# A vision-transformer block on one core: padded small products, other instruction orders, and both normalisations moved from VectorE to ScalarE

## The reference

```python
h = x.reshape(8, 1024, 29) @ tok_W + positions                 # 128 channels
z = layernorm(h)                                               # (h - mean) / sqrt(var + eps)
Q, K, V = (split_heads(z @ W + b) for W, b in ...)             # 8 heads of 16
attn = softmax((Q @ K.T + causal_mask) / 4)
h = h + (attn @ V) @ Wo + bo
y = layernorm(layernorm(h)) * ln_scale + ln_bias               # the second one inside the feed-forward part
shared = swiglu(y @ shared_in.T) @ shared_out.T + shared_out_b
# routing: argmax over 2 groups, softmax over the group's 4 experts, the top 2 of them, renormalised
routed = sum_e comb[:, e] * (swiglu(y @ expert_in.T) @ expert_out[e].T) + counts @ expert_out_bias
out = h + shared + routed
```

## Time and profile before

| | before |
|---|---|
| median of 3 runs | 1126.03 us |
| the profiled execution | 1126.66 us, its span 1124.9 us |
| granted TensorE clock, mean | 0.972 |
| TensorE busy | 1024.5 us (91%), 5632 products |
| VectorE busy | 787.9 us (70%) |
| ScalarE busy | 602.6 us (54%) |
| GpSimd busy | 324.3 us (29%) |
| DMA, mean over the span | 31 GB/s |

### The profile page before, as it was taken

One profiled execution on the slowest core, in us unless ns is written; L12 is line 12 of the kernel. 1 busy time (PEld: TensorE's weight loads), 2 busy tenths in 40 slices (PEclk: granted clock), 3 DMA queues, 4 the chain that ended last, 5 costly groups with the idle time before them and its releaser, 6 DMA issues.

```text
span 1124.9 us, 17182 instructions
## 1 busy us (share of the span) xinstructions
PE 1024.5 (91%) x5632; PEld 673.1 (60%) x5632; DVE 787.9 (70%) x2438; ACT 602.6 (54%) x1363; POOL 324.3 (29%) x466
## 2 busy tenths in 40 slices
PE   2688998999989998999989999999989999899966
PEld 1444665666657665676657665675656666576544
DVE  4578667785778767976687857877668857887133
ACT  1124654466645765556644666557644566457633
POOL 5211313123232323224132233313232232222233
PEclk9999999899989999999999999999989999999989
DMA  3520224004130044002140042200350040400000
GB/s 115 72 32 2 30 32 69 1 1 68 25 46 1 1 69 69 2 1 47 23 70 1 2 69 39 32 1 16 55 69 1 1 64 13 59 1 2 10 10 9
DMA packets 28808, 34.66 MB, mean 31 GB/s; under 512 B 5418, under 2 KB 15568, under 8 KB 28592
## 3 DMA queue, kind: packets, MB, share of 16 engines
q1 hardware_dynamic: 28720, 33.57, 19.7%
HBM read 3.61 MB, written 4.19 MB: 7 GB/s over the span
## 4 chain that ended last, share of the span: by engine, by line
PE 71%; DVE 11%; ACT 6%; DMA 4%; issue 3%; SPq 3%; POOL 1%; ACTq 0%; POOLq 0%; DVEq 0%
PE bank_p L495 13%; PE bank_s L470 13%; PE bank_w L513 10%; PE bank_f L598 4%; PE bank_f L600 4%; DVE mx_far L682 4%; PE bank_f L599 4%; PE bank_m L564 3%; SPq L366 2%; PE bank_f L418 2%; ACT sel_act L995 2%; PE bank_f L420 2%; PE bank_f L419 2%; DMA q_stack<-mrow_l 2%; ACT pt L933 2%
## 5 line engine op out<-in xcount | busy, mean ns | idle before, releaser
L933 ACT ACTIVATE pt<-bank_p 128x512 f32<-128x512 f32 (+3 forms) x768 | 353.6, 490 | 299.6 <-PE bank_p L495 282.4
L470 PE MATMUL bank_s<-k_stack,q_stack 112*128 112x512 f32 (+3 forms) x768 | 285.8, 404 | 30.0 <-DMA q_stack<-qk_l 10.2
L686 DVE CUSTOM_DVE_ANT_0 bank_s<-bank_s,causal 128x384 f32<-128x384 f32 (+3 forms) x512 | 246.9, 505 | 89.8 <-PE bank_s L470 83.9
L495 PE MATMUL bank_p<-q_stack,k_stack 128*128 128x512 f32 (+3 forms) x768 | 262.4, 385 | 14.6 <-ACT pt L933 14.0
L470 PEld LDWEIGHTS bank_s<-k_stack,q_stack 112*128 112x128 f32 x768 | 150.2, 201 | 134.5 <-DVE mx L686 68.4
L495 PEld LDWEIGHTS bank_p<-q_stack,k_stack 128*128 128x128 f32 x768 | 141.5, 194 | 114.4 <-ACT pt L933 90.1
L682 DVE TENSOR_REDUCE mx_far<-bank_s 128x1 f32<-128x512 f32 x256 | 166.4, 684 | 43.6 <-PE bank_s L470 42.4
L1070 POOL TENSOR_SCALAR_AFFINE_SELECT pt<-pt 128x512 f32<-128x512 f32 x128 | 81.1, 636 | 384.8 <-ACT pt L933 384.8
L513 PE MATMUL bank_w<-pt,v 128*32 128x512 f32 (+3 forms) x1536 | 162.9, 500 | 0.0
L598 PE MATMUL bank_f<-wex_h,hid_h 128*128 128x512 f32 x256 | 103.7, 405 | 1.3 <-DVE gate_dve L827 0.8
L600 PE MATMUL bank_f<-wex_h,hid_l 128*128 128x512 f32 x256 | 101.2, 395 | 0.0
(11 more groups left out here) (124 smaller groups left out, 1338.1 us busy)
## 6 DMA issues: line engine op xcount, KB each, us to landing
q_stack<-qk_h SPq DMA_DIRECT2D x64, 128.0 KB, 4.1
k_stack<-qk_h SPq DMA_DIRECT2D x64, 128.0 KB, 5.8
q_stack<-qk_l SPq DMA_DIRECT2D x32, 128.0 KB, 5.2
k_stack<-qk_l SPq DMA_DIRECT2D x32, 128.0 KB, 5.8
out<-h SPq DMA_DIRECT2D x16, 256.0 KB, 2.3
pt<-w_expert SPq DMA_DIRECT2D x1, 1024.0 KB
x_sb<-x_t SPq DMA_DIRECT2D x16, 58.0 KB
pos_sb<-pos SPq DMA_DIRECT2D x1, 512.0 KB
```

The lines of the kernel that those rows point to most:

```text
L470: nc.tensor.matmul(s_bank[s % 2][:, 0:cols], q_stack[0:STACK, half, hd, t % HT * P:(t % HT + 1) * P], k_stack[0:STACK, hd // 2, key_place( ...
L495: nc.tensor.matmul(p_bank[p % 2][:, q0:HALF], k_stack[:, hd // 2, key_place(i, kt // HT), kt % HT * P:(kt % HT + 1) * P], q_stack[:, half, ...
L686: nc.vector.tensor_tensor_reduce(src, src, causal[:, HALF - cols:HALF], 1.0, -3.0e38, ALU.add, ALU.max, mx[:, col:col + 1]).then_inc(s_tak ...
L933: nc.scalar.activation(pt[:, k % PT_SLOTS, j, q0:HALF], p_bank[p % 2][:, q0:HALF], ACT.Exp, scale=0.25).then_inc(exp_done, 1)
```

## The change

- **Orders.** `FIRST`, `WEAVE` and `LAST` take the place of the one table: one order for the first two periods together, one for each of the six full ones, one for the last two together. All strings are new, on all five engines.
- **Steps.** The statistics (`stat1`, `stat2`) and the normalising (`z1`, `z2`) become steps of their own, and routing comes in five pieces where it had three.
- **Normalisations.** ScalarE makes `z` and `z2` as `scale * token + shift` with the scale `rs` and the shift `-mean * rs` per token. GpSimd makes the negated mean and the shift, two more small instructions for each half and norm.
- **Values.** `v` is a split product of three fp32r matmuls per tile (12 of 128 columns) where it was a plain fp32 one (4 matmuls, 8 instructions); `zt` and its copy go.
- **Padding.** `x_sb`, `tokw_sb` are padded with zero rows to 128 partitions, the transposes of the maxima and counts to 128 columns, and the counts of four tiles go through one transpose and one fp32 product of 512 columns with a block-diagonal bias in place of four of each.
- **Buffers.** `pt` has three slots; `gate_act` and `gate_dve`, and `sel_act` and `sel_dve`, become one buffer each.
- **Beginning.** The position table comes in two halves, and TensorE no longer waits for it; ScalarE zeroes half of `q_stack` with four copies; VectorE makes the other new constants.

```diff
-PT_SLOTS = 2
+PT_SLOTS = 3
...
-    PROGRAM[engine] = [(n + image_of(st), st) for n in range(-2, B) for st in period(WEAVE[engine], streams())
-                       if 0 <= n + image_of(st) < B]
+    PROGRAM[engine] = woven(FIRST[engine], -2, -1)
+    for n in range(0, B - 2):
+        PROGRAM[engine] += woven(WEAVE[engine], n)
+    PROGRAM[engine] += woven(LAST[engine], B - 2, B - 1)
...
-                        mm = nc.tensor.matmul(m_bank[:, t * P:(t + 1) * P], zt[:, t * P:(t + 1) * P], wv_sb[:],
-                                              start=True, stop=True)
+                        tok = slice(t * P, (t + 1) * P)
+                        mm = split_mm(m_bank[:, tok], zt_h[:, tok], zt_l[:, tok], wqkv_h[:, 2, :], wqkv_l[:, 2, :])
...
-                nc.tensor.transpose(m_bank[0:ROWS, 0:P], mx[:, u * ROWS:(u + 1) * ROWS], ident[:]).then_inc(m_ready, 1)
+                nc.tensor.transpose(m_bank[:, 0:P], mx[:, u, :], ident[:]).then_inc(m_ready, 1)
...
-                    for t in range(HT):
-                        mm = nc.tensor.transpose(m_bank[0:EXPERTS + 1, t * P:(t + 1) * P], cnt[:, half * HT + t, :],
-                                                 ident[:])
+                    mm = nc.tensor.transpose(m_bank[:, 0:P], cnt[:, tiles(half), :].rearrange("p t e -> p (t e)"), ident[:])
...
-                    for t in range(HT):
-                        nc.tensor.matmul(m_bank[:, t * P:(t + 1) * P], cnt_t[:, t * P:(t + 1) * P], wbias_sb[:],
-                                         start=(t == 0), stop=False)
+                    nc.tensor.matmul(m_bank[:], cnt_t[:], wbias_sb[:], start=True, stop=False)
...
-                if kind == "turn1":
-                    dve.wait_ge(rs_made, n + 1)
-                    if n:
-                        dve.wait_ge(m_ready, after(half_before(i, half)[0], "turn1", 1 - half))
-                    for t in range(HT):
-                        nc.vector.tensor_scalar(z[:, t, :], h[:, slot(i, half), t, :], mv[:, t, 0:1], rs1[:, t:t + 1],
-                                                ALU.subtract, ALU.mult).then_inc(z_made, 1)
...
+                if kind == "z1":
+                    act.wait_ge(rs_made, (n + 1) * LN_STEPS)
+                    if n:
+                        act.wait_ge(m_ready, after(half_before(i, half)[0], "turn1", 1 - half))
+                    for t in range(HT):
+                        nc.scalar.activation(z[:, t, :], h[:, slot(i, half), t, :], ACT.Identity, bias=shift1[:, t:t + 1],
+                                             scale=rs1[:, t:t + 1]).then_inc(z_made, 1)
+                    return
...
-                    nc.scalar.copy(zt[:], m_bank[:]).then_inc(zt_made, 1)
...
+                    pool.wait_ge(rs_made, n * LN_STEPS + 1)
+                    nc.gpsimd.tensor_tensor(shift1[:], minus_mean1[:], rs1[:], ALU.mult).then_inc(rs_made, 1)
```

More of the change, by code:

```diff
@@ L24 @@
 GATE_W = 32
+CNT_W = 32
+XROWS = 32
 ODD = 64
@@ L67, in image_of @@
 def image_of(st):
-    if st[0] in ("emb", "turn1", "ztl", "q", "k", "v", "queries", "keys"):
+    if st[0] in ("emb", "stat1", "z1", "turn1", "ztl", "q", "k", "v", "queries", "keys"):
         return 2
@@ L150, in period, with woven @@
+def woven(weave, *periods):
+    joined = {}
+    for n in periods:
+        for name, stream in streams(n).items():
+            joined.setdefault(name, []).extend((n + image_of(st), st) for st in stream if 0 <= n + image_of(st) < B)
+    left = {name: iter(stream) for name, stream in joined.items()}
     return [next(left[name]) for name in weave]
@@ L724, in post @@
                                             ALU.add).then_inc(m_taken, 1)
-                    dve.wait_ge(m_taken, after(i, *st))
+                if kind == "stat2":
+                    mine = h[:, slot(i, half), :, :]
+                    dve.wait_ge(m_taken, after(i, "oproj", half))
                     for t in range(HT):
@@ L938, in post @@
                 n = half_no(i, half)
+                if kind == "z2":
+                    act.wait_ge(ln2_step, (n + 1) * LN2_STEPS)
+                    if n:
+                        act.wait_ge(m_ready, after(half_before(i, half)[0], "z2t", 1 - half))
+                    for t in range(HT):
+                        nc.scalar.activation(z2[:, t, :], h[:, slot(i, half), t, :], ACT.Identity, bias=shift2[:, t:t + 1],
+                                             scale=rs2[:, t:t + 1]).then_inc(z2_made, 1)
                 if kind == "ant":
@@ L1014, in stage @@
                     forward(i, st)
-                elif st[0] in ("ant", "z2t", "route", "counts"):
+                elif st[0] in ("z2", "ant", "z2t", "route", "counts"):
                     post(i, st)
+            act.wait_ge(keys_zeroed, 1)
+            zeros = words(k_stack[:, 0, :, :])
+            for n in range(0, HEADS, 2):
+                nc.scalar.copy(q_stack[:, 1, n:n + 2, :], zeros[:, 0:2, :]).then_inc(stacks_zeroed, 1)
             act.wait_ge(w_in1, 7 * 16)
@@ L1098, in combine @@
                 done = (i * TILES + t) * COMBINE
-                four, two = sel_act[:, t % 2, :], sel_dve[:, t % 2, 0:2 * P]
+                four, two = sel[:, t % 2, :], sel[:, t % 2, 0:2 * P]
                 mine = h[:, slot(i, t // HT), t % HT, :]
```

301 lines of the change are left out of this document (197 added, 104 removed).

## The result

The changed kernel takes 1079.57 us (median of 4 runs, 1078.65 to 1080.92), the kernel before 1126.27 in the same runs (1125.79 to 1127.19): the ratio is 0.9585, 95% interval 0.9569 to 0.9602. The forecast was 1086, so 6.4 us of the 46.7 us gained were missing from it. The profiled execution took 1080.25 us, its span 1078.4.

The account below looks back on a forecast made before the run. The prediction took TensorE's ordered list with its hand-overs as the bound. Start -3.5, image 0 -7.2, six periods -24.0, image 7 -3.3 and tail -2.2 sum to -40.2 from 1126.7, stated as 1086 us, range 1055 to 1121.

Parts of the forecast that it names:

- Relief of VectorE: Each period: VectorE's load falls by 4.9 of 97 us, so TensorE waits less for maxima, -1.5 us.
- ScalarE's blocks: Each period: four blocks of normalising, about 1.6 us each, stand before exponentials but are mostly covered, +0.7 us.
- the slower rival: Normalising blocks on ScalarE delay the exponentials TensorE waits for, up to 8.0 us per image: 1148 us, chance 0.13.
- Order: Border of two images: more `expert` products in TensorE's list hide 1.0 us more of its waits, -1.0 us per period.
- the pieces: Each period: split statistics, normalising and routing let VectorE put a maximum between, -0.5 us.
- Third slot: Each period: a third `pt` slot saves ScalarE's waits and lets `weigh` stand later in TensorE's list, -1.0 us.
- Clock: Each period: shorter waits, fuller operands and fewer tiny products could keep the clock up, -1.0 us, bounds 0 and 4.
- Products: TensorE's changed value, bias and transpose products: 0 to +0.25 us per half, +2 us in all, bounds -8 and +9.
- Image 0: Image 0's stage: half of its 7.9 us excess goes, plus 0.82 of a period's gain, -7.2 us.
- Start: Start: table load and `zt` copy leave the path, first `z` quicker, half 1's `z` off VectorE, -3.5 us.
- Tail: Tail: an `expert` step moves, the norm's chain lengthens, routing pieces and clock help, -2.2 us.

Follow-up runs that it names:

- ninth run: Kernel before, with the far maxima reading only 368 of 512 columns (less work for VectorE): 1127.84 us, ratio 1.0022.
- tenth run: Changed kernel, with the far maxima reading only 368 of 512 columns (less work for VectorE): 1072.84 us, ratio 0.9516.
- seventh: Changed kernel, with the next image's first maxima sent before half 1's queries and six `prob` started among the `expert` steps: 1083.15 us, ratio 0.9605.
- eighth: Changed kernel, with only the transpose and DMAs of the next image's first maxima moved earlier, `prob` left in place: 1081.83 us, ratio 0.9597.
- second run: Changed kernel with the orders of before and both normalisations on VectorE, but three `pt` slots: 1129.68 us, ratio 1.0022.
- fifth: Changed kernel with both normalisations back on VectorE, the new orders otherwise kept: 1101.56 us, ratio 0.9758.
- first run: Changed kernel with the orders of before, both normalisations on VectorE and two `pt` slots: 1128.45 us, ratio 0.9995.
- the filler: Changed kernel plus 16 unread products of 128 columns in TensorE's wait at each of the seven borders: 1073.15 us, ratio 0.9528.
- the fourth: Kernel before with one edit, values as three fp32r matmuls per tile and the copy `zt` gone: 1130.52 us, ratio 1.0026.

## Why the prediction was right, and where it wasn't

The forecast of 1086 holds as a sum, and that it came so near was in part luck: the six periods gained 13.7 us more than forecast, the other four stages 7.4 less. The main mechanism was named (TensorE's ordered list and its hand-overs bind, and the orders, the norms and the clock together ease them), but most of its terms had the wrong size.

- **Relief of VectorE, -1.5 per period.** The step "VectorE's load falls by 4.9 of 97, so a share of the waits for its maxima goes" was wrong as a rule. By itself the relief is worth 0 with the old orders (ninth run) and at most 6.7 / 8 = 0.8 per image with the new ones (tenth run, part of it clock). The move of the norms as a whole costs 39 us with the old orders and gives 22 with the new.
- **ScalarE's blocks, +0.7 per period, and the slower rival.** The block is 1.65 us long, as said (1.6). Whether it fits isn't a matter of idle time: ScalarE had 55 of 130 us idle, and in the old orders the same blocks still made TensorE wait. The rival's time, 1148, is on the side of the 1169 measured there; it didn't happen because the orders were new on all engines.
- **Order, -1.0 at the border and -0.5 for the pieces.** This is the mis-sized term. With the norms on VectorE on either side, the new steady order takes a period from 130.7 to 125.4 us, -5.3, and with the norms on ScalarE from 135.5 to 124.1. I had looked for its worth at the border, where the seventh and eighth runs find nothing to gain. What goes with the new orders in every run is some 30 us less of waiting for exponentials all along the period, in pieces of mostly under 1 us, and fewer falls of the clock (39.9 us at the lower level in six periods of the second run, 13.8 in the fifth, so at most 2.2 of the 5.3). That these waits are the gain isn't shown. The earlier trace rows had shown those 90.1 us; I had no way to price an order against them, and put the part that I could see.
- **Third slot, -1.0 per period.** Zero by itself, with the old orders: the wait for `weigh` went from 13.4 us to nothing between the first and the second run without moving the end. With the new orders 4.9 us of it are left, where the prediction had it gone.
- **Clock, -1.0 per period.** It gave at most 2.0, inside the bounds of 0 and 4, and more is to be had, as the filler showed.
- **Products, +2 in all.** The first run finds 0 for them with buffers and beginning (between -3.0 and +1.8 us), the fourth +3 for the values alone, at equal clock, so it is inside the bounds of -8 and +9.
- **Image 0, -7.2.** Half of the 7.9 us excess was to go; the excess has rather grown, to 9.8 against the new pace. The ends' own orders brought 3.4 there, or a higher clock did.
- **Start, -3.5.** The first block of `z` did fall from 2.82 to 1.65 us and the table load left the path, but the first score started only 1.2 us earlier, since it still waits for the keys' DMA. ScalarE's next instruction behind the table load starts only at 6.51 us, after a wait for VectorE, so no drain behind the load can be read from this trace.

```profile
0.78 1.28 ACT L1117 ACT_TABLE_LOAD   x1 [0.78 <-PEq L1303]
...
15.54 1.65 ACT L991 ACTIVATE z<-h,shift,rs 128x128 f32<-128x128 f32 x4 [5.15 <-POOL shift L1162]
...
38.16 0.66 PE L556 MATMUL bank_s<-k_stack,q_stack 112*128 112x128 f32 x2 [2.13 <-DMA k_stack<-qk_h]
```

- **Tail, -2.2.** Measured -1.7, so the size fits. Its parts don't come out: with one order for all the tail is 5.0 us longer, but with 10 us more at the lower clock level, so what the order of `LAST`, the norm's longer chain and the pieces of routing give or take is not told apart.

Not settled: which swaps of the new steady order make the gain. The runs undo the order as a whole. The products, the merged buffers and the split of statistics and routing were not undone under the new orders, so a share of theirs there isn't excluded.

## What to carry to other kernels

Where every engine follows a written order, an engine's load and its order can't be priced apart: taking 38 us off the second-busiest engine changed nothing, and moving them to a half idle engine cost 39 us, while with new orders the same move gained 22. Before pricing a move by "relief", take the same load away by itself in a copy of the kernel; if nothing happens, that engine's load isn't what binds under this order. And compare executions at the same granted clock before a few us are put down to an edit. A long gap on one engine, here 9.5 us without an exponential, is no bound by itself: look at which engine is full just behind it.

## What the runs showed of the hardware

In the changed kernel a TensorE wait of 1.8 to 2.0 us at full clock is followed, 0.2 to 2.0 us after it ends, by 3.4 us at the lower level at five of the six borders that have it; filled with 16 products of 128 columns (0.12 us each) it was at none. But the wait alone doesn't decide it: the run with one order for all periods has a wait of 1.8 to 2.1 us at all seven borders, and falls at only two. A scale and a shift per partition cost an activation of 128 columns 481 to 484 ns against 273 for a plain exponential of that size in the same trace:

```profile
L1022 ACT ACTIVATE pt<-bank_p 128x128 f32<-128x128 f32 x128 | 32.0, 273 | 34.6 <-PE bank_p L583 32.8 <-PE bank_w L601 1.5
```
